# Mixer decays in one GpSimd instruction per batch and head, without VectorE's clamp pass

## The reference

```python
def _segsum(a):
    s = jnp.cumsum(a, axis=-1)
    diff = s[..., :, None] - s[..., None, :]
    mask = jnp.tril(jnp.ones((c, c), dtype=bool))
    return jnp.where(mask, diff, -jnp.inf)
proj = jnp.einsum('bsd,ed->bse', x, in_proj_w)        # gate, hBC, dt
hBC  = silu(causal depthwise conv of width 4 over hBC) # hs, Bm, Cm
dt   = jnp.clip(jax.nn.softplus(dt + dt_bias), 0.0, 100.0)
A_dt = dt * -jnp.exp(A_log)                           # never positive
L    = jnp.exp(_segsum(A_dt))                         # decays, one 128 x 128 matrix per batch and head
Y    = jnp.einsum('bzlhn,bzshn,bhzls,bzshp->bzlhp', Cc, Bc, L, hs * dt) + hs * D
g    = Y * silu(gate)
out  = (g * rsqrt(mean(g*g over the group) + eps) * norm_w) @ out_proj_w.T
```

## Time and profile before

| | before |
|---|---|
| runs, median (lowest to highest) | 2916.17 us (2915.06 to 2918.78) |
| span of the profiled execution | 2919.1 us |
| TensorE matmul busy, mean granted clock | 2603.7 us (89%), 0.956 of full |
| VectorE busy | 1872.9 us (64%) |
| ScalarE busy | 1371.7 us (47%) |
| GpSimd busy | 1129.4 us (39%) |
| the decays: diff L1122, clamp L1217, exp L1023, scores L1233 | 128 instructions each |

### The profile page before, as it was taken

The page is one execution under the profiler, slowest core; times in us unless marked ns, Lnnn a source line. Parts: engine busy times, 40 slices in busy tenths (PEclk is TensorE's granted clock), DMA queues, the critical chain, the costliest instruction groups (busy, mean ns, idle before and its releaser), DMA issues. The chain is left out here.

```text
span 2919.1 us, 43490 instructions
## 1 busy us (share of the span) xinstructions
PE 2603.7 (89%) x14432; PEld 2118.4 (73%) x14432; DVE 1872.9 (64%) x3011; ACT 1371.7 (47%) x2589; POOL 1129.4 (39%) x889
## 2 busy tenths in 40 slices
PE   6677489999999999999999998699999999999958
PEld 4335377777777777777777776588888888888846
DVE  4565468688696886968859687454644645546453
ACT  2221156465464664646646464344544544545431
POOL 0000047565575655756557465322122221221210
PEclk9888789999999999999999998799999999999989
DMA  2100033032130321303213030101000000010010
GB/s 77 63 0 1 15 113 126 30 130 80 61 120 30 130 80 55 126 30 126 84 55 126 29 130 22 54 26 30 14 24 26 18 25 22 22 29 18 11 50 30
DMA packets 61999, 163.47 MB, mean 56 GB/s; under 512 B 8304, under 2 KB 8944, under 8 KB 53424
## 3 DMA queue, kind: packets, MB, share of 16 engines
q1 hardware_dynamic: 59232, 157.16, 15.9%
q10 hardware_dynamic: 2640, 4.47, 0.5%
HBM read 158.98 MB, written 2.62 MB: 55 GB/s over the span
## 5 line engine op out<-in xcount | busy, mean ns | idle before, releaser
L157 PE MATMUL bank<-XH,d_w_hi 128*128 128x512 f32 x1160 | 472.5, 407 | 32.8 <-POOL d_w_lo L1097 17.9
L159 PE MATMUL bank<-XH,d_w_lo 128*128 128x512 f32 x1160 | 458.7, 395 | 0.0
L158 PE MATMUL bank<-XL,d_w_hi 128*128 128x512 f32 x1160 | 457.1, 394 | 0.0
L1097 POOL TENSOR_TENSOR d_w_lo<-d_w,d_w_hi 128x512 fp32r<-128x512 f32 x144 | 223.9, 1555 | 322.8 <-ACT d_w_hi L982 322.7
L1200 DVE SCALAR_TENSOR_TENSOR d_hs<-bank,d_conv,d_hs 128x508 f32<-128x508 f32 (+2 forms) x384 | 279.5, 740 | 43.5 <-ACT d_hs L1003 34.5
L157 PEld LDWEIGHTS bank<-XH,d_w_hi 128*128 128x128 f32 x1160 | 220.4, 190 | 91.0 <-issue 25.4
L1122 POOL TENSOR_TENSOR d_decay<-d_decay,d_acg 128x1024 f32<-128x1024 f32 x128 | 270.3, 2132 | 0.0
L159 PEld LDWEIGHTS bank<-XH,d_w_lo 128*128 128x128 f32 x1160 | 220.3, 190 | 49.7
L158 PEld LDWEIGHTS bank<-XL,d_w_hi 128*128 128x128 f32 x1160 | 220.9, 190 | 44.1
L1127 POOL TENSOR_TENSOR d_gated_lo<-d_gated,d_gated_hi 128x512 fp32r<-128x512 f32 x128 | 165.7, 1297 | 206.2 <-ACT d_gated_hi L1031 206.2
L1233 DVE TENSOR_TENSOR d_decay<-d_decay,d_cb 128x1024 f32<-128x1024 f32 x128 | 181.3, 1457 | 76.4 <-ACT d_decay L1023 76.4
(11 more groups left out here) (282 smaller groups left out, 6689.1 us busy)
## 6 DMA issues: line engine op xcount, KB each, us to landing
d_decay<-running_sums SPq DMA_DIRECT2D x64, 1024.0 KB, 4.8
d_w<-in_L_w_groups SPq DMA_DIRECT2D x144, 256.0 KB, 3.5
e_w<-in_L_w_heads SPq DMA_DIRECT2D x80, 256.0 KB, 2.6
d_wo<-in_L_wo_groups SPq DMA_DIRECT2D x64, 256.0 KB, 4.8
X<-in_x SPq DMA_DIRECT2D x8, 256.0 KB, 9.1
b_ctx<-in_ctx SPq DMA_DIRECT2D x8, 256.0 KB, 5.6
e_ctx<-in_ctx SPq DMA_DIRECT2D x8, 256.0 KB, 2.7
out<-X SPq DMA_DIRECT2D x8, 256.0 KB, 2.0
```

The source lines that it names most:

```text
L157: pe.matmul(out, wh, xh, start=first, stop=False)
L158: pe.matmul(out, wh, xl, start=False, stop=False)
L159: return pe.matmul(out, wl, xh, start=False, stop=last)
L1097: pool.tensor_tensor(WL[:, w, :, :], WR[:, w, :, :], WH[:, w, :, :].bitcast(F32), ALU.subtract).then_inc(q["w_split"], 1)
```

## The change

`diff` now works batch by batch and head by head: 16 instructions TENSOR_SCALAR of 128x128 for each tile, each subtracting a per-partition scalar (one column of `ACG`) and then taking the minimum with 0. The last of each eight increments `diff`. `clamp`, its semaphore `clamped` and its three calls are gone, and `exp` waits for `diff`. A new counter `diff_begun` is incremented before the sixteen; nothing waits for it.

```diff
-                          "cb_ready clamped hs_turned y_ready ... tap cb diff xdt scores ..."
+                          "cb_ready hs_turned y_ready ... tap cb diff xdt diff_begun scores ..."
...
                 def exp(g, j):
                     for h in range(2):
-                        act.wait_ge(q["clamped"], START + 2 * (g * JT + j) + h + 1)
+                        act.wait_ge(q["diff"], START + 2 * (g * JT + j) + h + 1)
...
+                    pool.sem_inc(q["diff_begun"], 1)
                     for h in range(2):
-                        r = R[:, j % 2, :, tokens(h)].rearrange("p e (b t) -> p e b t", b=4)
-                        a = ACG[:, 4 * h:4 * h + 4, 2 * j:2 * j + 2].rearrange("p b (e o) -> p e b o", o=1)
-                        pool.tensor_tensor(r, r, a.broadcast_to([P, 2, 4, S]), ALU.subtract).then_inc(q["diff"], 1)
+                        for b in range(4 * h, 4 * h + 4):
+                            for e in range(2):
+                                r = R[:, j % 2, e, b * S:(b + 1) * S]
+                                last = pool.tensor_scalar(r, r, ACG[:, b, 2 * j + e:2 * j + e + 1], 0.0,
+                                                          ALU.subtract, ALU.min)
+                        last.then_inc(q["diff"], 1)
...
-                def clamp(g, j):
-
-                    for h in range(2):
-                        v.wait_ge(q["diff"], START + 2 * (g * JT + j) + h + 1)
-                        r = R[:, j % 2, :, tokens(h)]
-                        v.tensor_scalar(r, r, 0.0, None, ALU.min).then_inc(q["clamped"], 1)
-
...
                         conv(g, 4 + 2 * j)
-                        clamp(g, j + 1)
                         gated(g, j)
```

More of the change, by code:

```diff
@@ L806, in stage_mixer @@
         q = sems(c, "d_", "w_hi w_split wo_scaled wo_hi wo_split nw conv_par d_par tok_par conv_ready gate_ready "
-                          "cb_ready clamped hs_turned y_ready out_ready ssq_ready evac silu gate exp "
-                          "g_hi g_sq sq_sum tap cb diff xdt scores skip gated var acc g_lo rstd")
+                          "cb_ready hs_turned y_ready out_ready ssq_ready evac silu gate exp "
+                          "g_hi g_sq sq_sum tap cb diff xdt diff_begun scores skip gated var acc g_lo rstd")
         c.begin_at_start(q)
@@ L1293, in group @@
                         conv(g + 1, 2)
-                        clamp(g + 1, 0)
                         v.wait_ge(q["skip"], START + 2 * (g + 1) * JT)
@@ L1305, in _ @@
                     conv(0, i)
-                clamp(0, 0)
                 cb_mask(0)
```

## The result

The changed kernel takes 3237.7 us, the median of 4 runs (3233.98 to 3239.53), against 2917.5 us (2915.06 to 2919.75, 4 runs beside it): a ratio of 1.110 with a 95% interval of 1.108 to 1.112. It is 320 us slower. Forecast were 16 us less, with a range up to 2960.

The account below looks back on a forecast made before the run. TensorE was taken as the bound, VectorE binding by only 0.37 us in some iterations. Sum: -15 (a) - 4 (the turn) + 3 for what was left out = -16 us, from 2916.2 to 2900; range 2890 to 2960.

Parts of the forecast that it names:

- (a): TensorE's short waits before the scans in iterations 2 to 5 of a group, put down to VectorE: 15 us would go.
- the turn: Passage from one group to the next: VectorE some 2 us earlier shortens the norm sum's 5.6 us wait; 4 us gained.
- The ring: Loop of GpSimd's w_lo, diff, w_lo, wo and ScalarE's wo_hi, exp, w_hi: needs 13.55 us, 13.85 after the change.
- the 0.45 us of wo: GpSimd's L1108 takes 1.49 us beside VectorE's clamp and 1.04 without; the difference was to return to GpSimd.
- 0.45 of diff's 0.97 us: GpSimd's diff takes 4.78 us beside scores, 3.8 alone; about 0.45 us was to return as scores ends earlier.
- The price of the new instruction: GpSimd's TENSOR_SCALAR of 128x128 in diff: 0.31 us each, 5.0 us a tile.
- The high end: Top price of a new GpSimd instruction, two reads for each element: 435 ns, 7.0 us a tile, giving 2979 us.
- The slower rival: GpSimd's loop becomes the bound, from 0.36 us an instruction: +29 us, 2945 us at 6.3 us a tile; chance 0.36.
- four iterations: Iterations of a group outside the double ones: at 6.3 us a tile 0.58 us more each, 2.3 us a group.
- double ones: Two iterations a group where GpSimd prepares two output weights: forecast no loss; at 6.3 us a tile, 1.25 and 0.6.
- are not late by 1.2 us: At the turn, weights behind diff on GpSimd's list: no delay, as their products come an item or more later on TensorE.
- Short GpSimd instructions can hold it by 0.3 us at most: At the turn, VectorE's two-input product L1250, held up to 1.65 us by diff, would be held by 0.3 at most.

Follow-up runs that it names:

- e_noclamp: The kernel before without VectorE's clamp (nothing is clamped, exp runs with scale 0): 2893.7 us, ratio 0.992.
- e_two: The changed kernel with a tile's 16 instructions joined to two of 128x1024 that subtract an immediate 1.0 and clamp: 2992.7 us, ratio 1.026.
- e_half: The changed kernel with 8 of each tile's 16 instructions, the second head's decays neither subtracted nor clamped: 2933.4 us, ratio 1.006.
- e_split: The kernel before, clamp kept, with its two TENSOR_TENSOR a tile split into 16 of 128x128: 2993.5 us, ratio 1.027.
- m1_prices: The kernel before with unneeded GpSimd instructions of several forms and sizes heading its first stage; pointer TENSOR_SCALAR with two operations took 0.69 us at 128 elements.

## Why the prediction was wrong, point by point

- **What bounds the kernel: right.** VectorE held the iteration at 14.56 us by a hair; without its clamp it repeats in 14.00 (e_noclamp). The gain of the clamp, forecast as 15 us for (a) and 4 for the turn, was measured as 24. TensorE's own need was put at 14.20 us and is 14.00.
- **The ring, 13.55 us plus what diff takes over 3.8, less 0.9: right as a mechanism, and closer in its sums than it deserved.** With the measured 11.55 us it gives 20.4, and the iteration takes 20.35. With 7.2 (e_two) it gives 16.05, and 15.98 were measured. With 5.94 (e_half) it gives 14.8, and 14.82 were measured. But the 13.55 us were read from an iteration in which diff took 4.78 us, so a measured duration has to be set against 4.78, as e_split does, and only the 0.45 us of wo comes back: 19.9, 15.5 and 14.3 us, all about 0.5 short. Most of what is missing is the w_lo ahead of diff, which takes 2.00 us in the changed kernel and 1.57 before (at 657.72): in the changed kernel that w_lo, and no longer diff, runs beside scores (705.99 to 708.35). The forecast had 0.45 of diff's 0.97 us return; all of it did, and w_lo became 0.43 longer. The two errors cancel, and that is luck.
- **The price of the new instruction: wrong, and this is the step that failed.** "Its slope, if one element is read in each step: MEMSET of 128x128 against 128x2" gave 0.8 ns an element and 0.31 us. Measured are 3.4 ns an element, and 0.72 us. The high end, 0.435 us, was built from TENSOR_TENSOR's slope, on the thought that nothing which reads one operand can be slower than what reads two. m1_prices shows that it can: 2.6 ns with one operation, 3.4 with two, against 1.7. The trace of before had no TENSOR_SCALAR on GpSimd of more than one element, so neither end was an end. The range up to 2960 left out even the 2979 us that the forecast's own high end gave. The rows used, MEMSET and the affine select, are other operations of which nothing says that they share its speed.
- **The pointer: a small part.** 0.08 us an instruction, 1.3 us a tile.
- **From the price to the time.** The slower rival had the right place and the right rule. Its sum with 11.55 us: four iterations at +5.8 us, double ones at 7.75 - 1.25 = 6.5 and 7.75 - 1.9 = 5.85, 35.6 us a group, 285 in all. In the trace a group repeats in 222.4 us where it took 183.4 (from GpSimd's diffs of tile 1 at 579.35 and 762.72 before, 625.55 and 847.94 after): 39 us, 312 in all. The four iterations give 24.7 us and the double ones 5.9 and 4.8. The turn is where the sum was short: from the diff of tile 0 to that of tile 1 it is 70.9 us where it was 66.9. That the weights "are not late by 1.2 us" was right: with a diff of 5.94 or 7.2 us (e_half, e_two) the same stretch takes 64.8 and 65.2 us. At 7.7 us more it costs about 4 us a group.
- **"Short GpSimd instructions can hold it by 0.3 us at most": off with the price.** The longest of VectorE's products with the gate (L1250 before, L1247 after) took 1.82 us before and 2.31 after, beside one of the short instructions and the w_lo behind it, where one alone takes 0.69. It mattered little: 16 of the 128 took over 1.2 us before and 4 after, and scores in the changed kernel takes 1.22 us (two in 2.36), as it is over before diff begins.
- **`diff_begun`: no run isolates it.** Diff starts at 709.49 as the w_lo before it ends (707.51 + 2.00), so there is little room for it to matter.

## What to carry to other kernels

Price an instruction by a row of the same engine and the same operation at the size in question, or measure it. Where there is none, one list of instructions in an idle stretch gives the whole table, and the range must not be closed by a neighbour of another operation. Then look for rings: two engines that both stand idle part of the time can still be the bound when they hand work to each other in turn, and what counts is the time to spare in the ring, found by the wait that ends last. When a step is moved in such a ring, follow the queue of the engine that answers it too. And a small pass that must go somewhere is best put where an engine stands waiting: the clamp was free on ScalarE, while the change that put it on GpSimd, with the split into sixteen, cost 320 us. The clamp alone on GpSimd, as a second instruction, was not run.

## What the runs showed of the hardware that was not expected

- GpSimd's TENSOR_SCALAR is slower for each element than its TENSOR_TENSOR: 2.6 ns with one operation and 3.4 with two, against 1.7 with a broadcast operand, 0.9 for COPY. At 128x512 that is 1.49 (immediate, one operation) and 2.00 us (pointer, two) against 1.04 and 0.61. Why it is slower no run shows.
- From start to start, a TENSOR_TENSOR of 128x128 took 0.35 us with an output of its own and 0.39 in place (e_split, without the first of the sixteen); TENSOR_SCALAR 0.69 and 0.72. Whether it is the place or the surroundings was not told apart.
- The granted clock of TensorE was 0.92 in an iteration of the changed kernel in which it stood 4.56 us, and 1.00 in one of before, in which it stood 0.37; over the whole span 0.921 against 0.956. The first group of part 5 shows it too, L157's mean is 445 ns where it was 407. Inside the iteration the clock falls behind the stand: TensorE stands from 697.51 to 702.07, in the window from 702.00 to 704.00 the granted clock is 0.53, near the lower of its two levels (1.2 GHz of 2.4), and matmuls start 0.43 us apart; from 706.00 to 708.00 it is 1.00 and they start 0.23 apart. In the ring TensorE had time to spare, so at the full clock it would have waited longer by as much, and this should have cost nothing there; no run isolates it.
